# Attention projections as three fp32r products of high and low parts in place of fp32 matmuls

## The chip, the cores and the metric

The kernel runs on one core of a Trainium2 chip. The metric is the device time of one execution in microseconds (us). The profile is of one execution on that core.

## What is computed

The input x has 32 sequences of 256 tokens of width 128. Three layers follow each other, each on the normalised output of the one before and added to it: an expert FFN (weight 0.5), a differential attention, and the same FFN again. The attention, cut to what matters:

```python
q = (x @ Wq.T + bq)   # 256 wide: 16 heads, two streams of 8
k = (x @ Wk.T + bk)   # likewise
v = (x @ Wv.T + bv)   # 128 wide: 16 heads of 8
q1, q2, k1, k2 = rope of the halves of q and k
a1, a2 = softmax(causal(q1 k1^T * scale)), softmax(causal(q2 k2^T * scale))
out = (a1 - lam * a2) @ v
out = out * rsqrt(mean(out^2) + 1e-6) * head_norm_w * (1 - LAMBDA_INIT)
return out @ Wo.T + bo
```

## The kernel before, in words

`build` runs `ffn`, `attention` and `ffn` one after the other. Each is a block of five instruction streams (SyncE's DMA queue, GpSimd, ScalarE, VectorE, TensorE), written out by hand, with semaphores between them. There is no planner: an engine does its work in the order of its code.

The attention goes through the 32 sequences in turns. In a turn, work for several sequences is interleaved: the table `ORDER` lists 33 units of TensorE's work, and `offset(kind, u)` says which sequence a unit is for (+1 is the next one, -3 the third one back). All engines walk `ORDER` in the same way, and `AFTER` says behind which unit an engine does its further pieces of work. Each unit's result goes to one of three PSUM buffers of 1024 columns, `ring[:, pos % 3]`, where `pos` is its place in `ORDER`. `free` makes TensorE wait until the unit three places back has been read; so the pace of one unit is tied to the reader of another.

The units, in the order that matters here, are

```python
ORDER = [("XT", 0), ("T", 6), ("QK", 0), ("NM", 0), ("QK", 1), ("S", 0), ("S", 1), ("T", 7), ("T", 8), ("S", 2),
         ...
         ("S", 6), ("S", 7), ("T", 0), ("V", 0), ("T", 1), ("T", 2), ("NT", 0), ("NT", 1), ("OT", 0), ("S", 8),
         ...
```

- XT turns the normalised input (two 128x128 transposes, L1250). ScalarE copies it to `xt` in SBUF (L996).
- QK 0 and QK 1 are the projections of queries and of keys: four products each, with 128 stationary columns of `wqk` and the 256 columns of `xt` streaming (`mm`, L1223). VectorE reads them in four pieces of 256 columns, adding the bias and multiplying by the rotation (`turned`, L1087). GpSimd and ScalarE split the result in three bf16 parts, and DMAs stack them.
- V is the projection of values: two products, with 128 columns of `xt` stationary and the 128 columns of `wv` streaming. VectorE adds the bias (L1096).
- S is a set of scores whose row maximum VectorE takes (L1108); T is the same scores turned, to which ScalarE applies the exponential (L1002). In the timeline, an S unit is `att_kd,att_qs` with `att_hide`, and a T unit `att_qs,att_kd` with `att_hide_t`.
- "weigh 0" to "weigh 3" are 32 small matmuls each of the probabilities with the values (L1238), and NT turns their result back for VectorE (L1291 and L1116 on). NM turns the maxima (L1304).

An fp32 matmul shows in the trace as two instructions. The FFNs already do their large products with fp32r parts: `PRODUCTS = ((0, 0), (0, 1), (1, 0))` is high times high, high times low and low times high, the high part being a ScalarE copy to fp32r and the low part what VectorE or GpSimd subtracts. In the trace an fp32r operand of a matmul is written f32 as well; the names of the tiles tell them apart.

Before the turns there is a setup: DMAs bring weights and constants, VectorE clears keys and computes `stream_w` (L1184), TensorE waits for masks and weights. The projection of sequence 0 then comes in a turn of its own.

## Time and profile before

| | |
|---|---|
| time, median of 3 runs (lowest to highest) | 1902.27 us (1902.24 to 1903.05) |
| the profiled execution | 1901.86 us, its span 1900.0 us |
| mean granted clock of TensorE | 0.976 |
| TensorE busy | 1700.9 us (90%) |
| VectorE, ScalarE, GpSimd busy | 1368.9, 1275.2, 1048.1 us |

The span is from the first to the last instruction; what the profiled execution's time has beside it lies around it. The attention's first instructions start at about 436 us, and its steady turns run to about 1400 us. Starts are given in us from the span's start. Engines: PE is TensorE's matmuls, PEld its weight loads, DVE VectorE, ACT ScalarE, POOL GpSimd, SP the queue that issues the DMAs. Matmuls overlap, so a record's length is longer than its share of the stream: the distance of two starts tells the pace.

### The profile page before, as it was taken

What the parts mean: (1) busy time and instruction counts of PE and PEld (TensorE: products, weight loads), DVE (VectorE), ACT (ScalarE), POOL (GpSimd) and SP (SyncE); (2) the same over time, 40 slices, a digit from 0 to 9 for tenths busy, and PEclk for the clock granted to TensorE, in tenths of its full rate; (3) what the DMA queues carried; (4) which work ended last, traced back from release to release, by engine and by line L of the source; (5) the groups of instructions that cost most, each with busy time, mean ns of one, the idle gap of its engine ahead of it and who ended that gap; (6) DMA issues with size and microseconds to landing.
All of it is one profiled execution on the core that took longest, in us unless ns stands there. A gap on an engine that the chain in (4) does not pass through costs nothing. (4 is left out here: it accounts for less than half of the span.)

```text
span 1900.0 us, 43151 instructions
## 1 busy us (share of the span) xinstructions
PE 1700.9 (90%) x16448; PEld 1233.5 (65%) x16448; DVE 1368.9 (72%) x3442; ACT 1275.2 (67%) x1613; POOL 1048.1 (55%) x703
## 2 busy tenths in 40 slices
PE   4999999993699999999999999999975599999999
PEld 3778777772456656666666666666643487777787
DVE  5777777765877777777777777777751577777775
ACT  4777777771266676766767666676765577777776
POOL 4888888874333433434334343333411688888885
PEclk9999999996899999999999999999998799999999
DMA  3333333222322323233232322323211223333331
GB/s 111 101 112 112 112 112 101 85 90 80 81 63 78 84 60 92 59 85 82 61 92 58 85 77 68 92 54 89 73 28 51 90 99 111 112 106 107 112 107 62
DMA packets 142434, 163.14 MB, mean 86 GB/s; under 512 B 13218, under 2 KB 124018, under 8 KB 141042
## 3 DMA queue, kind: packets, MB, share of 16 engines
q1 hardware_dynamic: 142228, 160.38, 28.0%
q8 instruction: 131, 2.15, 0.5%
q14 instruction: 75, 0.61, 0.1%
HBM read 91.20 MB, written 14.70 MB: 56 GB/s over the span
## 5 line engine op out<-in xcount | busy, mean ns | idle before, releaser
L1002 ACT ACTIVATE att_prob<-att_ring 128x1024 f32<-128x1024 f32 x384 | 389.1, 1024 | 190.6 <-PE att_ring L1223 185.7
L292 POOL TENSOR_TENSOR ffn_h_low<-ffn_h,ffn_h_high 128x1024 fp32r<-128x1024 f32 x192 | 458.8, 2403 | 95.0 <-ACT ffn_h_high L341 94.8
L1108 DVE TENSOR_REDUCE att_nmax<-att_ring 128x4 f32<-128x1024 f32 (+1 forms) x384 | 454.0, 1218 | 73.0 <-PE att_ring L1223 72.4
L479 DVE TENSOR_TENSOR ffn_h<-ffn_up,ffn_comb_wide 128x1024 f32<-128x1024 f32 x256 | 311.3, 1216 | 125.0 <-ACT ffn_up L334 122.7
L334 ACT ACTIVATE ffn_up<-ffn_up 128x1024 f32<-128x1024 f32 x256 | 258.1, 1008 | 202.8 <-PE ffn_up L567 201.0
L341 ACT ACTIVATE ffn_h_high<-ffn_h 128x1024 fp32r<-128x1024 f32 x256 | 269.3, 1052 | 0.7 <-DVE ffn_h L479 0.7
L918 POOL TENSOR_TENSOR att_qk<-att_turned 128x512 f32<-128x512 f32 x64 | 81.5, 1273 | 321.2 <-DVE att_turned L1087 321.2
L567 PE MATMUL ffn_up<-ffn_xt_high,ffn_w_high 128*128 128x512 f32 x512 | 214.6, 419 | 1.6 <-DVE ffn_h L479 1.5
L580 PE MATMUL ffn_y<-ffn_h_high,ffn_w_high 128*128 128x512 f32 x512 | 205.5, 401 | 7.3 <-POOL ffn_h_low L292 6.0
L284 POOL TENSOR_TENSOR ffn_ez<-ffn_e_const,ffn_nz 128x16 f32<-128x16 f32 x64 | 185.8, 2904 | 38.2 <-DVE ffn_nz L405 38.2
L567 PE MATMUL ffn_up<-ffn_xt_low,ffn_w_high 128*128 128x512 f32 x512 | 203.5, 397 | 0.0
L567 PE MATMUL ffn_up<-ffn_xt_high,ffn_w_low 128*128 128x512 f32 x512 | 203.3, 397 | 0.0
L580 PE MATMUL ffn_y<-ffn_h_low,ffn_w_high 128*128 128x512 f32 x512 | 201.6, 394 | 0.0
L580 PE MATMUL ffn_y<-ffn_h_high,ffn_w_low 128*128 128x512 f32 x512 | 200.0, 391 | 0.0
L1223 PE MATMUL att_ring<-att_qs,att_kd 64*128 64x256 bf16 (+1 forms) x2048 | 150.4, 246 | 52.6 <-DVE att_nmax L1108 29.4
L1238 PE MATMUL att_o_ps<-att_prob,att_v 128*32 128x256 f32 (+1 forms) x4096 | 194.2, 331 | 0.0
L1223 PE MATMUL att_ring<-att_hide,att_eye 64*128 64x256 bf16 (+1 forms) x1536 | 176.2, 308 | 0.0
L1223 PE MATMUL att_ring<-att_hide_t,att_eye 64*128 64x256 bf16 (+1 forms) x1536 | 174.5, 306 | 0.0
L1223 PE MATMUL att_ring<-att_kd,att_qs 64*128 64x256 bf16 (+1 forms) x2048 | 150.7, 246 | 23.3 <-DVE att_nmax L1108 15.6
L1238 PEld LDWEIGHTS att_o_ps<-att_prob,att_v 128*32 128x32 f32 x4096 | 115.3, 110 | 85.9 <-ACT att_prob L1002 26.7
L1087 DVE SCALAR_TENSOR_TENSOR att_turned<-att_ring,att_bqk,att_rope 128x256 f32<-128x256 f32 x256 | 106.2, 477 | 80.4 <-PE att_ring L1223 80.4
L1223 PEld LDWEIGHTS att_ring<-att_qs,att_kd 64*128 64x128 bf16 x2048 | 64.2, 94 | 134.9 <-DVE att_nmax L1108 74.3
(142 smaller groups left out, 2826.8 us busy)
## 6 DMA issues: line engine op xcount, KB each, us to landing
ffn_comb_wide<-ffn_comb_d SPq DMA_DIRECT2D x128, 512.0 KB, 5.6
att_qs<-att_parts SPq DMA_DIRECT2D x192, 128.0 KB, 2.5
att_kd<-att_parts SPq DMA_DIRECT2D x192, 128.0 KB, 2.5
ffn_x<-x SPq DMA_DIRECT2D x32, 256.0 KB, 3.1
ffn_w<-w SPq DMA_DIRECT2D x4, 1024.0 KB, 7.2
x<-ffn_out SPq DMA_DIRECT2D x16, 256.0 KB, 2.4
att_x<-x SPq DMA_DIRECT2D x32, 128.0 KB, 2.3
att_xr<-x SPq DMA_DIRECT2D x32, 128.0 KB, 2.3
```

What stands on the lines that cost most here:

```text
L284: nc.gpsimd.tensor_tensor(ez[:, k].rearrange("p t e -> p (t e)"), e_const[:, 0:n], nz[:, k].rearrange("p t e -> p (t e)"), ALU.pow).then_i ...
L292: nc.gpsimd.tensor_tensor(hts[1][:, e % NH], h[:, e % NH], hts[0][:, e % NH], ALU.subtract).then_inc(low_by_pool, 1)
L334: nc.scalar.activation(up[:, e % NUP], up[:, e % NUP], ACT.Silu).then_inc(silu_ready, 1)
L341: nc.scalar.activation(hts[0][:, e % NH], h[:, e % NH], ACT.Copy).then_inc(high_ready, 1)
L479: nc.vector.tensor_tensor(h[:, e % NH], up[:, e % NUP], comb_wide[:, b.c % NW, e].unsqueeze(1).to_broadcast([P, HE, FT]), ALU.mult).then_i ...
L567: last = nc.tensor.matmul(up[:, e % NUP, k], w1s[a1][:, col:col + P], xts[a2][:, b.slot()], start=(n == 0), stop=(n == 2))
L580: last = nc.tensor.matmul(y[:], w2s[a1][:, col:col + D], hts[a2][:, e % NH, k], start=(e == 0 and k == 0 and n == 0), stop=(e == E - 1 and ...
L1002: nc.scalar.activation(prob[:, u % NP], ring[:, ORDER.index((kind, u)) % 3], ACT.Exp, scale=SCALE).then_inc(prob_ready, 1)
L1087: last = nc.vector.scalar_tensor_tensor(out=turned[:, u, partner, c * S:(c + 1) * S], in0=ring[:, pos % 3, col:col + S], scalar=bqk[:, n:n ...
L1108: nc.vector.tensor_reduce(nmax[:, b, :, h0:h0 + cnt], ring[:, pos % 3] .rearrange("p (s h k) -> p s h k", s=2, k=width), AX.X, ALU.max, ne ...
L1223: return nc.tensor.matmul(out, lhs, rhs, start=start, stop=stop)
L1238: last = nc.tensor.matmul(o_ps[VW * i:VW * (i + 1), g % 2, j, b * P:S], v[:, k, b, h], p, start=(b == 0), stop=(b == 1), tile_position=(0, ...
```

## The change

ScalarE's copy of the turned input goes to an fp32r tile, the high part. VectorE then subtracts it from the PSUM original, giving the low part, and TensorE's QK waits for that (`xt_low`) instead of for the copy. `wqk` and `wv` are split once in the setup, two copies on ScalarE and two subtractions on VectorE, and TensorE waits for these before its first transposes. Each product of QK and of V becomes three fp32r products accumulated in PSUM. The output projection `wo` (OP) stays in fp32.

```diff
--- before.py
+++ after.py
250.31 0.39 PE L567 MATMUL ffn_up<-ffn_xt_high,ffn_w_low 128*128 128x512 f32 x1
...
250.54 0.40 PE L580 MATMUL ffn_y<-ffn_h_high,ffn_w_high 128*128 128x512 f32 x1
...
252.04 0.19 PEld L547 LDWEIGHTS ffn_gate_ps<-ffn_gate_ws,ffn_xt_high 128*128 128x128 f32 x1
...
252.15 -736,7 +736,9 250.31 0.39 PE L567 MATMUL ffn_up<-ffn_xt_high,ffn_w_low 128*128 128x512 f32 x1
...
250.54 0.40 PE L580 MATMUL ffn_y<-ffn_h_high,ffn_w_high 128*128 128x512 f32 x1
...
252.04 0.19 PEld L547 LDWEIGHTS ffn_gate_ps<-ffn_gate_ws,ffn_xt_high 128*128 128x128 f32 x1
...
252.15
         var_eps = sb("var_eps", [P, QB])
         rstd = sb("rstd", [P, QB])
         xn = sb("xn", [P, QB, D])
-        xt = sb("xt", [P, S])
+        wqks = [sb(f"wqk_{n}", [P, 2 * NC4, P], F32R) for n in ("high", "low")]
+        wvs = [sb(f"wv_{n}", [P, D], F32R) for n in ("high", "low")]
+        xts = [sb(f"xt_{n}", [P, S], F32R) for n in ("high", "low")]
         turned = sb("turned", [P, 2, 2, 2 * S])
         qk = sb("qk", [P, 2, 2 * S])
         left = sb("left", [P, 2, 2 * S])
250.31 0.39 PE L567 MATMUL ffn_up<-ffn_xt_high,ffn_w_low 128*128 128x512 f32 x1
...
250.54 0.40 PE L580 MATMUL ffn_y<-ffn_h_high,ffn_w_high 128*128 128x512 f32 x1
...
252.04 0.19 PEld L547 LDWEIGHTS ffn_gate_ps<-ffn_gate_ws,ffn_xt_high 128*128 128x128 f32 x1
...
252.15 -791,6 +793,9 250.31 0.39 PE L567 MATMUL ffn_up<-ffn_xt_high,ffn_w_low 128*128 128x512 f32 x1
...
250.54 0.40 PE L580 MATMUL ffn_y<-ffn_h_high,ffn_w_high 128*128 128x512 f32 x1
...
252.04 0.19 PEld L547 LDWEIGHTS ffn_gate_ps<-ffn_gate_ws,ffn_xt_high 128*128 128x128 f32 x1
...
252.15
         ln_step = sem("ln_step")
         rstd_ready = sem("rstd_ready")
         xn_ready = sem("xn_ready")
+        weight_high = sem("weight_high")
+        weight_low = sem("weight_low")
+        xt_low = sem("xt_low")
         pe = {kind: sem(f"{kind}_computed") for kind in UNITS}
         read = {kind: sem(f"{kind}_read") for kind in UNITS}
         qk_ready = sem("qk_ready")
250.31 0.39 PE L567 MATMUL ffn_up<-ffn_xt_high,ffn_w_low 128*128 128x512 f32 x1
...
250.54 0.40 PE L580 MATMUL ffn_y<-ffn_h_high,ffn_w_high 128*128 128x512 f32 x1
...
252.04 0.19 PEld L547 LDWEIGHTS ffn_gate_ps<-ffn_gate_ws,ffn_xt_high 128*128 128x128 f32 x1
...
252.15 -982,6 +987,9 250.31 0.39 PE L567 MATMUL ffn_up<-ffn_xt_high,ffn_w_low 128*128 128x512 f32 x1
...
250.54 0.40 PE L580 MATMUL ffn_y<-ffn_h_high,ffn_w_high 128*128 128x512 f32 x1
...
252.04 0.19 PEld L547 LDWEIGHTS ffn_gate_ps<-ffn_gate_ws,ffn_xt_high 128*128 128x128 f32 x1
...
252.15
             @block.scalar
             def _(act):
 
+                act.wait_ge(weights_in, 16 * 12)
+                nc.scalar.activation(wqks[0][:], wqk[:], ACT.Copy).then_inc(weight_high, 1)
+                nc.scalar.activation(wvs[0][:], wv[:], ACT.Copy).then_inc(weight_high, 1)
                 act.wait_ge(dve_setup, 2)
                 nc.scalar.activation(ln_ms[:], y0[:], ACT.Ln).then_inc(lam_ready, 1)
                 act.wait_ge(lam_sums, 1)
250.31 0.39 PE L567 MATMUL ffn_up<-ffn_xt_high,ffn_w_low 128*128 128x512 f32 x1
...
250.54 0.40 PE L580 MATMUL ffn_y<-ffn_h_high,ffn_w_high 128*128 128x512 f32 x1
...
252.04 0.19 PEld L547 LDWEIGHTS ffn_gate_ps<-ffn_gate_ws,ffn_xt_high 128*128 128x128 f32 x1
...
252.15 -993,7 +1001,7 250.31 0.39 PE L567 MATMUL ffn_up<-ffn_xt_high,ffn_w_low 128*128 128x512 f32 x1
...
250.54 0.40 PE L580 MATMUL ffn_y<-ffn_h_high,ffn_w_high 128*128 128x512 f32 x1
...
252.04 0.19 PEld L547 LDWEIGHTS ffn_gate_ps<-ffn_gate_ws,ffn_xt_high 128*128 128x128 f32 x1
...
252.15
                             wait_unit(act, turn, kind, u)
 
                             wait(act, pe["V"], turn.at(0, 1, 1))
-                            nc.scalar.activation(xt[:], ring[:, ORDER.index((kind, u)) % 3, 0:S],
+                            nc.scalar.activation(xts[0][:], ring[:, ORDER.index((kind, u)) % 3, 0:S],
                                                  ACT.Copy).then_inc(read["XT"], 1)
                         if kind == "T" and turn.runs(offset(kind, u)):
                             wait_unit(act, turn, kind, u)
250.31 0.39 PE L567 MATMUL ffn_up<-ffn_xt_high,ffn_w_low 128*128 128x512 f32 x1
...
250.54 0.40 PE L580 MATMUL ffn_y<-ffn_h_high,ffn_w_high 128*128 128x512 f32 x1
...
252.04 0.19 PEld L547 LDWEIGHTS ffn_gate_ps<-ffn_gate_ws,ffn_xt_high 128*128 128x128 f32 x1
...
252.15 -1133,6 +1141,11 250.31 0.39 PE L567 MATMUL ffn_up<-ffn_xt_high,ffn_w_low 128*128 128x512 f32 x1
...
250.54 0.40 PE L580 MATMUL ffn_y<-ffn_h_high,ffn_w_high 128*128 128x512 f32 x1
...
252.04 0.19 PEld L547 LDWEIGHTS ffn_gate_ps<-ffn_gate_ws,ffn_xt_high 128*128 128x128 f32 x1
...
252.15
                             wait(dve, ms_ready, turn.at(-3, 1, 1))
                             nc.vector.tensor_scalar(ms_eps[:], ms[:], 1.0 / HD, RMS_EPS, ALU.mult,
                                                     ALU.add).then_inc(norm_step, 1)
+                        if kind == "XT" and turn.runs(1):
+
+                            wait(dve, read["XT"], turn.at(1, 1, 1))
+                            nc.vector.tensor_tensor(xts[1][:], ring[:, pos % 3, 0:S], xts[0][:],
+                                                    ALU.subtract).then_inc(xt_low, 1)
                         if (kind, u) == AFTER["newton"] and turn.runs(-3):
 
                             wait(dve, rms_step, turn.at(-3, 2, 2))
250.31 0.39 PE L567 MATMUL ffn_up<-ffn_xt_high,ffn_w_low 128*128 128x512 f32 x1
...
250.54 0.40 PE L580 MATMUL ffn_y<-ffn_h_high,ffn_w_high 128*128 128x512 f32 x1
...
252.04 0.19 PEld L547 LDWEIGHTS ffn_gate_ps<-ffn_gate_ws,ffn_xt_high 128*128 128x128 f32 x1
...
252.15 -1184,6 +1197,9 250.31 0.39 PE L567 MATMUL ffn_up<-ffn_xt_high,ffn_w_low 128*128 128x512 f32 x1
...
250.54 0.40 PE L580 MATMUL ffn_y<-ffn_h_high,ffn_w_high 128*128 128x512 f32 x1
...
252.04 0.19 PEld L547 LDWEIGHTS ffn_gate_ps<-ffn_gate_ws,ffn_xt_high 128*128 128x128 f32 x1
...
252.15
                 nc.vector.scalar_tensor_tensor(out=stream_w[:, :, 1], in0=by_head(1), scalar=-LAMBDA_INIT,
                                                in1=by_head(0), op0=ALU.add, op1=ALU.subtract).then_inc(lam_step, 1)
                 dve.wait_ge(lam_step, 3)
+                dve.wait_ge(weight_high, 2)
+                nc.vector.tensor_tensor(wqks[1][:], wqk[:], wqks[0][:], ALU.subtract).then_inc(weight_low, 1)
+                nc.vector.tensor_tensor(wvs[1][:], wv[:], wvs[0][:], ALU.subtract).then_inc(weight_low, 1)
                 dve.wait_ge(v_set, 1)
                 body(first.after())
                 clear_keys(1)
250.31 0.39 PE L567 MATMUL ffn_up<-ffn_xt_high,ffn_w_low 128*128 128x512 f32 x1
...
250.54 0.40 PE L580 MATMUL ffn_y<-ffn_h_high,ffn_w_high 128*128 128x512 f32 x1
...
252.04 0.19 PEld L547 LDWEIGHTS ffn_gate_ps<-ffn_gate_ws,ffn_xt_high 128*128 128x128 f32 x1
...
252.15 -1197,6 +1213,7 250.31 0.39 PE L567 MATMUL ffn_up<-ffn_xt_high,ffn_w_low 128*128 128x512 f32 x1
...
250.54 0.40 PE L580 MATMUL ffn_y<-ffn_h_high,ffn_w_high 128*128 128x512 f32 x1
...
252.04 0.19 PEld L547 LDWEIGHTS ffn_gate_ps<-ffn_gate_ws,ffn_xt_high 128*128 128x128 f32 x1
...
252.15
                 te.wait_ge(masks_in, 16 * 3)
                 tile = [slice(TILE * s, TILE * (s + 1)) for s in range(2)]
                 te.wait_ge(weights_in, 16 * 12)
+                te.wait_ge(weight_low, 2)
 
                 def free(turn, pos):
 
250.31 0.39 PE L567 MATMUL ffn_up<-ffn_xt_high,ffn_w_low 128*128 128x512 f32 x1
...
250.54 0.40 PE L580 MATMUL ffn_y<-ffn_h_high,ffn_w_high 128*128 128x512 f32 x1
...
252.04 0.19 PEld L547 LDWEIGHTS ffn_gate_ps<-ffn_gate_ws,ffn_xt_high 128*128 128x128 f32 x1
...
252.15 -1212,7 +1229,9 250.31 0.39 PE L567 MATMUL ffn_up<-ffn_xt_high,ffn_w_low 128*128 128x512 f32 x1
...
250.54 0.40 PE L580 MATMUL ffn_y<-ffn_h_high,ffn_w_high 128*128 128x512 f32 x1
...
252.04 0.19 PEld L547 LDWEIGHTS ffn_gate_ps<-ffn_gate_ws,ffn_xt_high 128*128 128x128 f32 x1
...
252.15
                         if before.runs(offset(kind, u)):
                             break
                         back -= 3
-                    if kind == "T":
+                    if kind == "XT":
+                        wait(te, xt_low, before.at(1, 1, 1))
+                    elif kind == "T":
                         wait(te, prob_ready, before.at(offset(kind, u), 12, u + 1))
                     elif kind == "NT":
                         wait(te, norm_step, before.at(offset(kind, u), NORM, 3 * u + 3))
250.31 0.39 PE L567 MATMUL ffn_up<-ffn_xt_high,ffn_w_low 128*128 128x512 f32 x1
...
250.54 0.40 PE L580 MATMUL ffn_y<-ffn_h_high,ffn_w_high 128*128 128x512 f32 x1
...
252.04 0.19 PEld L547 LDWEIGHTS ffn_gate_ps<-ffn_gate_ws,ffn_xt_high 128*128 128x128 f32 x1
...
252.15 -1249,12 +1268,16 250.31 0.39 PE L567 MATMUL ffn_up<-ffn_xt_high,ffn_w_low 128*128 128x512 f32 x1
...
250.54 0.40 PE L580 MATMUL ffn_y<-ffn_h_high,ffn_w_high 128*128 128x512 f32 x1
...
252.04 0.19 PEld L547 LDWEIGHTS ffn_gate_ps<-ffn_gate_ws,ffn_xt_high 128*128 128x128 f32 x1
...
252.15
                                 for t in range(QB):
                                     last = nc.tensor.transpose(buf[:, t * P:(t + 1) * P], xn[:, t], ident[:])
                             elif kind == "QK":
-                                wait(te, read["XT"], turn.at(1, 1, 1))
+                                wait(te, xt_low, turn.at(1, 1, 1))
                                 for n in range(4):
-                                    last = mm(buf[:, n * S:(n + 1) * S], wqk[:, 4 * u + n], xt[:])
+                                    for i, (a1, a2) in enumerate(PRODUCTS):
+                                        last = mm(buf[:, n * S:(n + 1) * S], wqks[a1][:, 4 * u + n], xts[a2][:],
+                                                  start=(i == 0), stop=(i == 2))
                             elif kind == "V":
                                 for t in range(QB):
-                                    last = mm(buf[:, t * D:(t + 1) * D], xt[:, t * P:(t + 1) * P], wv[:])
+                                    for i, (a1, a2) in enumerate(PRODUCTS):
+                                        last = mm(buf[:, t * D:(t + 1) * D], xts[a2][:, t * P:(t + 1) * P], wvs[a1][:],
+                                                  start=(i == 0), stop=(i == 2))
                             elif kind == "S":
                                 k = turn.slot(0)
                                 if u == 0:
```

## Rows read from the trace of the kernel before

**Rows 1.** The page: busy time, share of the span and instructions of each engine.
```profile
PE 1700.9 (90%) x16448; PEld 1233.5 (65%) x16448; DVE 1368.9 (72%) x3442; ACT 1275.2 (67%) x1613; POOL 1048.1 (55%) x703
```

**Rows 2.** Windows of the attention: busy PE, PEld, DVE, ACT, POOL; granted clock; DMA.
```profile
1200.00:1300.00 100.00, 92.44 (x1309) 61.47 (x1310) 77.96 (x156) 69.13 (x90) 34.98 (x38) 1.00 0.28 74
```

**Rows 3.** Timeline of TensorE: the XT transposes of two turns, fifteen turns apart.
```profile
908.05 0.44 PE L1250 MATMUL att_ring<-att_ident,att_xn 128*128 128x128 f32 x2
...
1355.17 0.44 PE L1250 MATMUL att_ring<-att_ident,att_xn 128*128 128x128 f32 x2
```

**Rows 4.** Timeline of all engines, from the XT copy on: start, us, engine, line, [idle before <-releaser].
```profile
908.68 0.38 ACT L996 ACTIVATE att_xt<-att_ring 128x256 f32<-128x256 f32 x1
...
909.20 1.97 PE L1223 MATMUL att_ring<-att_xt,att_wqk 128*128 128x256 f32 x8 [0.17 <-ACT att_xt L996]
...
911.00 0.27 PE L1304 MATMUL att_ring<-att_ident,att_nmax_parts 128*96 128x128 bf16 x2
...
911.11 1.95 PE L1223 MATMUL att_ring<-att_xt,att_wqk 128*128 128x256 f32 x8
911.20 1.66 DVE L1087 SCALAR_TENSOR_TENSOR att_turned<-att_ring,att_bqk,att_rope 128x256 f32<-128x256 f32 x4 [2.24 <-PE att_ring L1223]
...
913.10 1.66 DVE L1087 SCALAR_TENSOR_TENSOR att_turned<-att_ring,att_bqk,att_rope 128x256 f32<-128x256 f32 x4 [0.24 <-PE att_ring L1223]
...
914.67 2.35 DVE L1108 TENSOR_REDUCE att_nmax<-att_ring 128x8 f32<-128x1024 f32 x2
...
914.81 0.39 PE L1223 MATMUL att_ring<-att_qs,att_kd 64*128 64x256 bf16 x4 [0.34 <-DVE att_turned L1087]
...
918.32 4.73 DVE L1108 TENSOR_REDUCE att_nmax<-att_ring 128x8 f32<-128x1024 f32 x4 [0.37 <-PE att_ring L1223]
```

**Rows 5.** The same timeline, from V to the reads of NT.
```profile
926.91 0.71 PE L1223 MATMUL att_ring<-att_wv,att_xt 128*128 128x128 f32 x4
...
927.93 0.49 DVE L1096 TENSOR_TENSOR att_v<-att_ring,att_bv 128x128 f32<-128x128 f32 x2
...
928.23 0.59 PE L1223 MATMUL att_ring<-att_hide_t,att_eye 64*128 64x512 bf16 x4
...
928.75 1.97 PE L1291 MATMUL att_ring<-att_ident,att_o_t 128*128 128x128 f32 x16
929.88 0.36 DVE L1116 RECIPROCAL att_rsum<-att_ring 128x32 f32<-128x32 f32 x1 [1.46 <-PE att_ring L1291]
```

**Rows 6.** Timeline of TensorE and its weight loads in the first FFN: fp32r products.
```profile
250.31 0.39 PE L567 MATMUL ffn_up<-ffn_xt_high,ffn_w_low 128*128 128x512 f32 x1
...
250.54 0.40 PE L580 MATMUL ffn_y<-ffn_h_high,ffn_w_high 128*128 128x512 f32 x1
...
252.04 0.19 PEld L547 LDWEIGHTS ffn_gate_ps<-ffn_gate_ws,ffn_xt_high 128*128 128x128 f32 x1
...
252.15 0.19 PEld L547 LDWEIGHTS ffn_gate_ps<-ffn_gate_ws,ffn_xt_low 128*128 128x128 f32 x1
```

**Rows 7.** VectorE's groups by line and shape: count, busy us, mean ns of one.
```profile
L487 DVE TENSOR_TENSOR ffn_h_low<-ffn_h,ffn_h_high 128x1024 fp32r<-128x1024 f32 x24 | 29.9, 1244 | 0.0
...
L395 DVE TENSOR_TENSOR ffn_xt_low<-ffn_turn_ps,ffn_xt_high 128x512 fp32r<-128x512 f32 x12 | 8.3, 692 | 17.2 <-ACT ffn_xt_high L322 17.2
...
L1127 DVE TENSOR_TENSOR att_xo<-att_ring,att_xrb 128x256 f32<-128x256 f32 x28 | 11.6, 415 | 0.0
```

**Rows 8.** Timeline of the attention's setup.
```profile
441.97 0.43 SPq L828 DMA_DIRECT2D att_lam_in<-lk  x1
...
454.19 0.18 DVE L1184 SCALAR_TENSOR_TENSOR att_stream_w<-att_lam_exp 128x16 f32<-128x16 f32 x1
...
454.48 5.26 PE L1223 MATMUL att_ring<-att_xt,att_wqk 128*128 128x256 f32 x16 [2.72 <-ACT att_xt L996]
458.17 3.27 DVE L1087 SCALAR_TENSOR_TENSOR att_turned<-att_ring,att_bqk,att_rope 128x256 f32<-128x256 f32 x8 [3.80 <-PE att_ring L1223]
```

**Rows 9.** Busy time by window, first QK projection: columns as in rows 2.
```profile
455.00:459.00 4.00, 4.00 (x14) 3.24 (x13) 0.83 (x3) 0.00 (x0) 0.00 (x0) 0.67 0.03 6
```

## Prediction

> **What bounds the kernel now.** I read first the page's busy shares [rows 1], then the busy time of each engine and the granted clock in the attention stage alone [rows 2]. The reader should see there that TensorE is the busiest engine (92 of 100 us), but that VectorE has 78 of 100 too, so neither can be taken as the bound over a whole turn. The granted clock is 1.00, the 2.4 GHz level, in the steady part. The stage is strictly periodic: the transposes of the turned input (XT) start at 908.05 in one turn and at 1355.17 fifteen turns later, 447.12 / 15 = 29.81 us a turn [rows 3]. Only what makes this period longer or shorter counts, some 28 times; the first three turns and the setup are to be costed apart.
>
> So I read the timeline of one turn around the edited lines [rows 4, 5] and asked in each place who waits last. From the XT copy on, TensorE computes QK 0 (909.20 to 911.17), VectorE starts to read it at once (911.20, after 2.24 us idle), TensorE computes QK 1 (ready 913.06), VectorE has read QK 0 at 912.86, waits 0.24 us and reads QK 1 until 914.76, and only then can TensorE start T 7 (914.81), whose PSUM buffer that was. From T 7 on TensorE runs through weigh 1, T 8 and S 2 with no gap to speak of, until VectorE, idle again, gets S 2 at 918.32 [rows 4]. Whatever moves T 7 moves the turn. The second place is V: it streams at 926.91, T 1 and T 2 follow, then the NT transposes at 928.75, and VectorE has been idle for 1.46 us when it starts on them at 929.88 [rows 5]. There TensorE is the path, so whatever V takes longer is lost. The V result itself has slack: it is ready at 927.62, and VectorE takes it at 927.93, being occupied until then with the statistics. Between these places the path lies on VectorE's maxima and on TensorE's weighing, which the change does not touch.
>
> **The change, part by part.** Times are those of the turn shown.
>
> *Queries and keys, duration.* Before, one fp32 product is recorded as two instructions, and 8 take 1.80 us from first start (909.20) to the start of what follows (911.00): 0.216 each, and 0.07 once, at the beginning. The result is there 0.17 us after the stream's end (911.17) [rows 4]. After, a unit has 12 fp32r instructions of 256 columns. No row has that shape. Lower bound: the loads of fp32r weights follow each other every 0.11 us in the gate's products, where only 16 columns stream (252.04, 252.15) [rows 6], so 0.111. Upper bound: fp32r with 512 columns follows every 0.23 us (250.31, 250.54) [rows 6], where 512 columns at 2.4 GHz are 0.213; if those 17 ns are a fixed cost, 256 columns take 0.107 + 0.017 = 0.124; if they are in proportion, 0.115. I take 0.117. The stream is 0.07 + 12 x 0.117 = 1.47 us instead of 1.80: -0.33 (bounds -0.40 and -0.25) for each unit.
>
> *Queries and keys, a later start.* The low part is a VectorE subtraction that stands between ACT's copy and the first product. The copy ends at 909.06 [rows 4]. VectorE has nothing to do then: its last piece before is the mean square, and what is queued behind the new wait is the read of QK 0 itself, so nothing else is held up. Its price: the same operation on 512 columns of PSUM takes 0.692 us, and an add of 256 columns from PSUM (L1127) 0.415; I take 0.42 [rows 7]. It starts 0.03 after the copy (as 911.20 stands to 911.17), ends at 909.51, and TensorE starts 0.07 to 0.14 later (0.05 at T 7, 0.14 at the present first product): first product 909.58 to 909.65, or +0.41 (0.38 to 0.45).
>
> *What comes out at T 7.* QK 0 is ready 0.41 - 0.33 = 0.08 later, so VectorE starts on it at 911.28. Its four reads take 1.57 when another operation follows without a wait (from 913.10 to the reduction that comes next, 914.67), so it can begin QK 1 at 912.85. TensorE has QK 1 at 911.08 (stream end) + 0.11 (NM) + 1.95 - 0.32 = 912.82. Both agree: the read begins at 912.86 instead of 913.10, **-0.24 us**. With the lower bounds of both terms -0.35; with the upper ones QK 1 is ready at 913.03 and the gain is -0.03. Of 0.65 us of stream saved in two units, then, 0.41 goes to the subtraction, and the rest is the 0.24 that VectorE now waits. S 0 is no limit: it needs QK 0's buffer, now free 0.08 later, and its reduction stands behind QK 1's in any case.
>
> *V.* 4 instructions become 6. With 128 columns the stationary loads set the pace: 4 of them and their set-in fill 926.91 to 927.56 [rows 5], and both kinds of load come every 0.11 us [rows 6]. So 2 x 0.111 = **+0.22 us**, with nothing to hide it, as said above; the result is then ready at 927.84, still ahead of VectorE's 927.93.
>
> *Sum of a turn:* -0.24 + 0.22 = -0.02, times 28 = -0.6 us. Bounds: -0.35 + 0.21 = -0.14 (-3.9 us), and -0.03 + 0.23 = +0.20 (+5.6 us).
>
> *Setup and cold turns.* ACT's two weight copies wait for the weights alone, whose last DMA is issued at 441.97 [rows 8]; ACT has nothing else that is needed before 453.9, so I cost them at nothing (if the weights were late, up to 1.3 us). VectorE's two subtractions come behind its last setup step, which ends at 454.37 [rows 8]: 1.24 for 1024 columns [rows 7] and about 0.2 for 128, until 455.85. TensorE now waits for them ahead of the first XT, which was hidden before. Transposes 0.66, copy 0.37, subtraction 0.42 and the gaps bring the first product to about 457.5 instead of 454.48: +3.0. The clock there is 0.67 and below [rows 9], so the 8 instructions took 458.17 - 454.48 = 3.69 us; 12 at half clock, 0.222 each, take about 3.1: -0.6. QK 1 hides behind VectorE. That leaves +2.4, and -0.2 for each of two more cold turns (+0.42 - 0.6): **+2.0 us**, between +1 (the POOL and DMA chain of the first turns takes up some) and +3.5.
>
> *Sum:* -0.6 + 2.0 = +1.4 on the profiled execution's 1901.86 (span 1900.0 and 1.9 around it) gives 1903.3; the median of the runs shown is 0.4 higher, so **1903.7**. By the bounds: -2.9 and +9.1, or 1899.4 to 1911.4.
>
> **The rivals.** A difference under 0.2% (3.8 us) is about what a measurement of this kernel can't tell from none.
>
> *V's narrow fp32r products are slow.* Nothing shows how fast fp32r streams with 128 columns; gate rows with 16 and FFN rows with 512 leave it open. If an instruction takes as long as a 256-column fp32 one, 0.216, V takes 6 x 0.216 + 0.2 instead of 0.65: +0.85, a net +0.61 us a turn, 28 x 0.61 + 2 = +19: 1921. It decides from 0.125 us an instruction on, where V's extra passes 0.30 and the turn's net (3.8 - 2) / 28 = 0.064. For it: only that the width is untried. Against: two widths ran without such a penalty. Chance 0.08.
>
> *The upper bounds hold (fixed cost, late wake-up).* QK gains 0.03 to 0.1, V costs 0.22: 28 x 0.15 + 2.5 = +6.7: 1909. Chance 0.2.
>
> *V's extra 0.22 us is absorbed (the other side).* If NT is in truth held by something other than the stream before it (the label on its idle load is VectorE's V read, 928.42, which is 0.33 ahead of 928.75), only the QK gain is left: 28 x -0.24 + 2.0 = -4.7: 1897.5. It needs 0.21 us a turn net to count as faster. Against: T 2's last four matmuls start at 928.23; of 512 columns each, two at a time, they stream 0.43 us at 2.4 GHz, so until 928.66, and NT follows 0.09 later [rows 5]. Chance 0.09.
>
> *TensorE's saving counts in full.* The Trainium skill, "FP8 and Floating Point Precision", section "TensorE Precision Notes", has true FP32 as four passes, so that three products would cost three quarters of it; the 256-column rows agree (two times 0.216 are four times 0.107). As a mechanism of this kernel: if all three projections fell to three quarters, 3.46 + 0.43 us a turn would fall by 0.97, less the subtraction 0.41: -0.56, times 28, +2 = -14: 1888.5. Against: V is bound by loads, and VectorE's back-to-back reads cap QK. Chance 0.02.
>
> *fp32r weights load faster in the attention.* If a load took half of 0.111, V's six instructions would take 0.33 us instead of 0.44, so -0.11 in place of +0.22, and the turn -0.35: 28 x -0.35 + 2 = -7.8: 1894.5. It decides from 0.079 an instruction down, where the turn's net passes -0.21. Against: the gate loads the same type and shape at 0.11 [rows 6]. Chance 0.01. The Trainium skill, "TensorE: Matmul & The Clock Gate", section "Weight-path perf modes", speaks for it: it has the fast weight load on for 128 weights of any type that is not FP32. By this rule, the trace does not agree for fp32r.
>
> *The forecast*, no measurable change, by the sum above: chance 0.60.
>
> **How the numbers follow.** The forecast is the likeliest case, 1903.7. Slower by over 0.2% (above 1906.1): the first two rivals, 0.28, and 0.02 for a dearer setup: 0.30. Faster (below 1898.5): 0.12 together, of which 0.02 may stay within: 0.10. Same: 0.60. The range 1899 to 1911, the bounds of the unknown costs, leaves out the slow V (0.08) and most of the three faster cases (0.10); the case of the upper bounds is inside.
>
> **What would show it.** Right: QK 0's twelve matmuls span about 1.6 us; first product some 0.4 us later after the XT copy; VectorE's wait between the QK reads gone; QK matmul starts 0.115 to 0.124 apart; V's group about 0.9 us long; the period 29.7 to 30.0; the first QK product near 457.5. Wrong: matmul starts in V over 0.13 apart, NT's distance to the S units before it unchanged, a period under 29.65, or a subtraction much longer than 0.42 because ACT's exponential reads PSUM beside it.

## The result, and the profile after

The change costs 7.8 us: a median of 1910.09 us (1909.79 to 1910.46, 6 runs) against 1902.26 us (6 runs), a ratio of 1.0038 with a 95% interval of 1.0025 to 1.0051. That is above the forecast of 1903.7 and inside its range of 1899 to 1911; the outcome is "slower by over 0.2%", to which 0.30 was given. The profiled execution has a span of 1908.7 us, 8.7 above the one before. (In the diff above, rows of the first FFN's timeline, those of [rows 6], stand where the line numbers of each piece belong; they are no part of the kernel.)

The page's busy shares answer to [rows 1]:

```profile
PE 1693.1 (89%) x16768; PEld 1245.2 (65%) x16768; DVE 1381.3 (72%) x3476; ACT 1276.0 (67%) x1615; POOL 1047.1 (55%) x703
```

The window of the steady turns, with the columns of [rows 2]:

```profile
1200.00:1300.00 100.00, 91.34 (x1362) 62.46 (x1360) 79.40 (x160) 66.83 (x88) 37.13 (x42) 1.00 0.32 85
```

TensorE's busy time falls by 7.8 us, and the program is longer by as much. The timeline of TensorE has the XT transposes of two turns, fifteen apart, to be laid beside [rows 3]:

```profile
914.94 0.44 PE L1269 MATMUL att_ring<-att_ident,att_xn 128*128 128x128 f32 x2
...
1362.55 0.44 PE L1269 MATMUL att_ring<-att_ident,att_xn 128*128 128x128 f32 x2
```

447.61 / 15 = 29.84 us a turn, +0.03. Over the steady turns that is under 1 us of the 8.7. So where are the others? The starts of XT, read from the same view of both executions, tell it:

| us from the span's start | before | after | difference |
|---|---|---|---|
| first XT | 451.11 | 455.88 | +4.77 |
| second XT | 468.69 | 471.38 | +2.69 |
| third XT | 494.35 | 500.25 | +5.90 |
| fifth XT | 550.35 | 556.84 | +6.49 |
| last XT | 1355.17 | 1362.55 | +7.38 |
| first instruction of the second FFN | 1464.69 | 1473.74 | +9.05 |
| end of the span | 1900.0 | 1908.7 | +8.7 |

Three quarters come ahead of the fifth XT: 2.7 us in the first projection and its chain, 3.2 us more from the second XT to the third, and 0.6 from there to the fifth. The steady turns add 0.9. After the last XT, where one QK and one V are all that is left of the changed code, 1.7 us are added.

The QK stretch of the turn at 914.94, all engines, answers to [rows 4]:

```profile
915.57 0.38 ACT L1004 ACTIVATE att_xt_high<-att_ring 128x256 fp32r<-128x256 f32 x1
...
915.98 0.43 DVE L1147 TENSOR_TENSOR att_xt_low<-att_ring,att_xt_high 128x256 fp32r<-128x256 f32 x1
...
916.55 0.36 PE L1242 MATMUL att_ring<-att_xt_high,att_wqk_high 128*128 128x256 f32 x1 [0.63 <-DVE att_xt_low L1147]
...
916.75 0.28 PE L1242 MATMUL att_ring<-att_xt_low,att_wqk_high 128*128 128x256 f32 x1
...
916.86 0.28 PE L1242 MATMUL att_ring<-att_xt_high,att_wqk_low 128*128 128x256 f32 x1
...
918.06 0.27 PE L1327 MATMUL att_ring<-att_ident,att_nmax_parts 128*96 128x128 bf16 x2
...
918.26 3.25 DVE L1095 SCALAR_TENSOR_TENSOR att_turned<-att_ring,att_bqk,att_rope 128x256 f32<-128x256 f32 x8 [1.86 <-PE att_ring L1242]
...
921.57 0.39 PE L1242 MATMUL att_ring<-att_qs,att_kd 64*128 64x256 bf16 x4
```

The reader should see three things. TensorE starts QK 0 at 1.61 us after XT (916.55 - 914.94) instead of 1.15, having waited for the subtraction. The whole unit streams until NM at 918.06, 1.51 us instead of 1.80, so QK 0 is with VectorE 0.17 us later after XT than before (3.32 against 3.15). And VectorE's eight reads are now one unbroken piece of 3.25 us, the 0.24 us of waiting between them gone. T 7 starts 6.63 after XT, before 6.76: 0.13 us are won.

V and the first NT transposes, which answer to [rows 5]:

```profile
933.67 0.33 PE L1242 MATMUL att_ring<-att_wv_high,att_xt_high 128*128 128x128 f32 x1
...
934.28 0.27 PE L1242 MATMUL att_ring<-att_wv_low,att_xt_high 128*128 128x128 f32 x1
...
934.68 0.49 DVE L1104 TENSOR_TENSOR att_v<-att_ring,att_bv 128x128 f32<-128x128 f32 x2
...
935.16 0.59 PE L1242 MATMUL att_ring<-att_hide_t,att_eye 64*128 64x512 bf16 x4
...
935.68 1.53 PE L1314 MATMUL att_ring<-att_ident,att_o_t 128*128 128x128 f32 x12
```

From V's start to NT's it is 2.01 us, before 1.84: the 0.17 us by which V is longer arrive in full at NT. -0.13 + 0.17 is the +0.03 of the period, but for the rounding of the starts.

The large new piece is in the second projection, at the start of the turns. VectorE and ScalarE there, and TensorE's first product:

```profile
471.61 1.76 DVE L1177 MEMSET att_kd<- 128x2048 uint32 x1 [0.38 <-issue]
472.08 0.38 ACT L1004 ACTIVATE att_xt_high<-att_ring 128x256 fp32r<-128x256 f32 x1 [3.71 <-PE att_ring L1269]
...
473.75 1.76 DVE L1177 MEMSET att_kd<- 128x2048 uint32 x1 [0.37 <-issue]
475.43 0.36 DVE L1147 TENSOR_TENSOR att_xt_low<-att_ring,att_xt_high 128x256 fp32r<-128x256 f32 x1
...
475.94 0.55 PE L1242 MATMUL att_ring<-att_xt_high,att_wqk_high 128*128 128x256 f32 x1 [3.90 <-DVE att_xt_low L1147]
```

The copy is ready at 472.46, but the subtraction stands in VectorE's queue behind two clears of key slots, and TensorE waits for it, 3.90 us in all; the first product is 4.56 us after XT (471.38). Before, the same clears ran beside the products, and the first product was 1.22 us after XT:

```profile
468.69 0.66 PE L1250 MATMUL att_ring<-att_ident,att_xn 128*128 128x128 f32 x2 [6.48 <-DVE att_xn L1067]
468.92 1.76 DVE L1164 MEMSET att_kd<- 128x2048 uint32 x1 [0.37 <-issue]
...
469.91 4.60 PE L1223 MATMUL att_ring<-att_xt,att_wqk 128*128 128x256 f32 x10 [0.56 <-ACT att_xt L996]
...
471.06 1.76 DVE L1164 MEMSET att_kd<- 128x2048 uint32 x1 [0.38 <-issue]
```

### The profile page after: what moved, and what is told of

It is laid out like the page before. It is cut to its first block and busy times, and to the rows that moved or that the text cites. A ratio compares the mean times of both kernels' runs of the same rounds, so it can differ in the third digit from the quotient of the medians.

```text
span 1908.7 us, 43829 instructions
## 1 busy us (share of the span) xinstructions
PE 1693.1 (89%) x16768; PEld 1245.2 (65%) x16768; DVE 1381.3 (72%) x3476; ACT 1276.0 (67%) x1615; POOL 1047.1 (55%) x703
```

## The experiments

All kernels below start from the changed kernel, except e5, which starts from the one before. Ratios are to the kernel before. "..." marks what is left out of an edit.

**e1: the key clears behind the subtraction**

```diff
                 body(first.after())
-                clear_keys(1)
-                clear_keys(2)
                 turns(body, 0)
...
                             nc.vector.tensor_tensor(xts[1][:], ring[:, pos % 3, 0:S], xts[0][:],
                                                     ALU.subtract).then_inc(xt_low, 1)
+                            if turn.c <= 0:
+                                clear_keys(turn.c + 2)
```

> The changed kernel, with VectorE's two clears of key slots 1 and 2 (1.76 us each) issued behind the low-part subtraction of the first two projections instead of ahead of the turns. Theory: most of the loss is there, because in the second projection the subtraction (475.43) stood in VectorE's queue behind both clears (471.61 to 475.5) while the copy was ready at 472.46. Then the second projection's first product comes some 3 us sooner relative to its XT (1.6 us after it instead of 4.56), and the time falls by about 3 us, from 1910.1 to 1907. Rival: the first turns are longer because the clock is at 1.2 GHz there and 24 loads cost as much as 16 long streams; then moving the clears gives under 0.5 us.

1906.74 us, ratio 1.0024 (1.0013 to 1.0034), 3.35 us less than the changed kernel. The theory's number. But the profiled execution was the longest of the eight (1912.06 us), and its fourth XT came 30.92 us after the third, where the changed kernel needs 26.98. So the same kernel was run once more.

**e9: the same kernel once more**

> The kernel with the key clears behind the subtraction once more, for another look at its first turns: in the profile already taken the distance from the third to the fourth XT was 30.92 us against 26.98 without the edit, while most of its timed runs were short. Theory: that is the clock's phase, and another execution has the third distance near 27 and the time near 1906.5. Rival: it is a wait that the edit brings, and both profiles have it.

1905.37 us, ratio 1.0017 (1.0007 to 1.0028), 4.7 us less than the changed kernel; the two medians of this one kernel differ by 1.4 us, so the 3.35 is not exact. Its second projection, TensorE, ScalarE and VectorE:

```profile
471.98 0.38 ACT L1004 ACTIVATE att_xt_high<-att_ring 128x256 fp32r<-128x256 f32 x1 [3.71 <-PE att_ring L1269]
472.40 0.42 DVE L1150 TENSOR_TENSOR att_xt_low<-att_ring,att_xt_high 128x256 fp32r<-128x256 f32 x1 [1.26 <-ACT att_xt_high L1004]
472.97 0.55 PE L1242 MATMUL att_ring<-att_xt_high,att_wqk_high 128*128 128x256 f32 x1 [1.02 <-DVE att_xt_low L1150]
```

The first product is 1.69 us after XT (471.28), as the theory said, and the third XT comes 25.52 after the second, where the changed kernel needs 28.87: 3.35 us less. In the execution of e1 it was 26.34, or 2.5 us less. From the third to the fourth it is 26.99 here (496.80 to 523.79). The same stretch in windows, for this execution (the last three columns are granted clock, DMA share and GB/s):

```profile
497.00:524.00 27.00, 19.49 (x236) 13.20 (x234) 21.62 (x39) 9.39 (x13) 7.68 (x7) 0.87 0.26 71
```

And for the execution of e1:

```profile
498.00:529.00 31.00, 23.75 (x236) 15.89 (x234) 21.89 (x39) 9.54 (x13) 7.68 (x7) 0.72 0.23 62
```

Equal work (236 matmuls, 39 VectorE instructions in both), a granted clock of 0.87 against 0.72, and 4.3 us more of TensorE's busy time for it (19.49 and 23.75). So the odd 30.92 goes with that execution's clock and not with the edit.

**e4: TensorE waits for the split weights at the first QK**

```diff
-                te.wait_ge(weight_low, 2)
...
                             elif kind == "QK":
+                                if turn.c == -1 and u == 0:
+                                    te.wait_ge(weight_low, 2)
                                 wait(te, xt_low, turn.at(1, 1, 1))
```

> The changed kernel with TensorE's wait for the split weights at the first QK instead of ahead of the first XT. Theory: the first XT is hidden again, VectorE goes from the weights' subtraction straight to the input's, and the first product comes at about 456.1 instead of 457.5: -1.4 us, 1908.7. Rival: the chain of GpSimd and DMAs behind the first projection takes it up, and the time stays at 1910.

1908.39 us, ratio 1.0028 (1.0017 to 1.0038), 1.7 less than the changed kernel. XT is hidden again, VectorE goes straight from the weights to the input, and the first product is at 456.04:

```profile
454.13 1.22 DVE L1201 TENSOR_TENSOR att_wqk_low<-att_wqk,att_wqk_high 128x1024 fp32r<-128x1024 f32 x1
455.28 0.28 DVE L1202 TENSOR_TENSOR att_wv_low<-att_wv,att_wv_high 128x128 fp32r<-128x128 f32 x1
455.48 0.42 DVE L1147 TENSOR_TENSOR att_xt_low<-att_ring,att_xt_high 128x256 fp32r<-128x256 f32 x1
456.04 0.55 PE L1241 MATMUL att_ring<-att_xt_high,att_wqk_high 128*128 128x256 f32 x1 [4.54 <-DVE att_xt_low L1147]
```

**e8: both edits of the start (e1 and e4)**

> The changed kernel with the two edits of its start alone: key clears behind the subtraction and the late wait for the split weights; the steady turns are untouched (29.84). Theory: they add, 3.35 + 1.7 measured one by one, so 1905.0; what then stands above the kernel before, about 2.5 us, is 28 times 0.03 and the lower clock of the first turns and the drain. Rival: both remove the same wait, and the time stays at 1906.5 or above.

1904.65 us, ratio 1.0017 (1.0007 to 1.0027), 5.4 less than the changed kernel and 3.7 less than e4: they add, as nearly as these medians can tell. What remains above the kernel before is 2.4 us.

**e2: V with two products**

This leaves out the product with the low part of V's weights.

```diff
                                 for t in range(QB):
-                                    for i, (a1, a2) in enumerate(PRODUCTS):
+                                    for i, (a1, a2) in enumerate(PRODUCTS[:2]):
...
-                                                  start=(i == 0), stop=(i == 2))
+                                                  start=(i == 0), stop=(i == 1))
```

> The changed kernel with two products for V instead of three (the low part of its weights is left out): 4 instructions as in the kernel before. Theory: V is on TensorE's path, and loads set its pace, so each turn loses 0.22 us: the period falls from 29.84 to 29.62 and the time by 28 x 0.22 = 6 us to 1904. Rival: V's extra time is absorbed ahead of NT, and the period stays within 0.05 of 29.84.

The period, from TensorE's timeline, is (1356.77 - 912.52) / 15 = 29.62:

```profile
912.52 0.44 PE L1269 MATMUL att_ring<-att_ident,att_xn 128*128 128x128 f32 x2
...
1356.77 0.44 PE L1269 MATMUL att_ring<-att_ident,att_xn 128*128 128x128 f32 x2
```

1902.32 us, ratio 1.0003 (0.9993 to 1.0012). Two instructions fewer of 0.11 us each take exactly 0.22 us off every turn. V's time is on the path. The time fell by 7.8 us, 1.6 more than 28 x 0.22; from the last XT to the second FFN this execution took 108.65 us, the one of the changed kernel 111.19, and of these 2.5 us the edit explains 0.22.

**e3: the low input's products last**

```diff
-                                wait(te, xt_low, turn.at(1, 1, 1))
-                                for n in range(4):
-                                    for i, (a1, a2) in enumerate(PRODUCTS):
-                                        last = mm(..., wqks[a1][:, 4 * u + n], xts[a2][:],
-                                                  start=(i == 0), stop=(i == 2))
+                                wait(te, read["XT"], turn.at(1, 1, 1))
+                                for i, (a1, a2) in enumerate(((0, 0), (1, 0), (0, 1))):
+                                    if i == 2:
+                                        wait(te, xt_low, turn.at(1, 1, 1))
+                                    for n in range(4):
+                                        last = mm(..., wqks[a1][:, 4 * u + n], xts[a2][:],
+                                                  start=(i == 0 and n % 2 == 0), stop=(i == 2 and n % 2 == 1))
```

(The four pieces are taken in pairs: an accumulation group is opened with the first piece of a pair and closed with the second, since their products now alternate.)

> The changed kernel with QK's products in another order: high times high and low weights times high input for all four pieces first, waiting only for ScalarE's copy, and only then the low input's products, behind the wait for the subtraction. Theory: the subtraction costs the path 0.46 us a turn (first product 1.61 after XT against 1.15 before the change), and 8 products of 0.12 cover it; the period falls by 0.46 to 29.38, the time by 28 x 0.46 = 13 us and a bit in the first turns, to 1896: faster than both kernels. Rival: VectorE's reads of QK and not the start of QK 0 set T 7; then the period moves by under 0.1.

1892.81 us, ratio 0.9948 (0.9931 to 0.9964): 9.7 us faster than the kernel before and 17.3 faster than the changed one. A turn of it, all engines:

```profile
904.80 0.44 PE L1269 MATMUL att_ring<-att_ident,att_xn 128*128 128x128 f32 x2
...
905.84 0.42 DVE L1147 TENSOR_TENSOR att_xt_low<-att_ring,att_xt_high 128x256 fp32r<-128x256 f32 x1
...
905.96 0.71 PE L1242 MATMUL att_ring<-att_xt_high,att_wqk_high 128*128 128x256 f32 x4 [0.17 <-ACT att_xt_high L1004]
906.51 0.64 PE L1242 MATMUL att_ring<-att_xt_high,att_wqk_low 128*128 128x256 f32 x4
906.98 0.64 PE L1242 MATMUL att_ring<-att_xt_low,att_wqk_high 128*128 128x256 f32 x4
...
907.66 3.25 DVE L1095 SCALAR_TENSOR_TENSOR att_turned<-att_ring,att_bqk,att_rope 128x256 f32<-128x256 f32 x8 [1.40 <-PE att_ring L1242]
...
910.97 0.39 PE L1242 MATMUL att_ring<-att_qs,att_kd 64*128 64x256 bf16 x4
```

The subtraction (905.84 to 906.26) lies beneath the first eight products, which run until 906.98. T 7 starts 6.17 after XT, not 6.63, and the period is (1345.51 - 904.80) / 15 = 29.38. All 0.46 us arrive.

That is 28 x 0.46 = 12.9 of the 17.3 us. Most of the others are won ahead of the fourth XT, which comes at 523.10 and not at 527.23. In the second projection the subtraction still stands behind the two clears, but eight products go ahead of it, and TensorE waits for it for 1.20 us instead of 3.90:

```profile
475.47 1.22 PE L1242 MATMUL att_ring<-att_xt_low,att_wqk_high 128*128 128x256 f32 x4 [1.20 <-DVE att_xt_low L1147]
```

From the third XT to the fourth 1.5 us are won as well; the granted clock was 0.94 there (497 to 524), and 0.87 in the changed kernel (500 to 527), so not all of that need be the edit's.

**e5: fp32 products and the subtraction alone**

The kernel before with one more VectorE operation, whose result nothing reads:

```diff
+                        if kind == "XT" and turn.runs(1):
+                            wait(dve, read["XT"], turn.at(1, 1, 1))
+                            nc.vector.tensor_tensor(xt_low_sb[:], ring[:, pos % 3, 0:S], xt[:],
+                                                    ALU.subtract).then_inc(xt_low, 1)
...
-                                wait(te, read["XT"], turn.at(1, 1, 1))
+                                wait(te, xt_low, turn.at(1, 1, 1))
```

> The kernel before, with fp32 projections, and beside them the new subtraction alone: VectorE writes the difference of the PSUM original and the copy to a tile that nothing reads, and QK waits for it as in the changed kernel. Theory: the subtraction is 0.46 us on the path of every turn, so the period rises from 29.81 to 30.27; in the second projection it stands behind the two key clears and costs 3.3 us more; 28 x 0.46 + 3.3 = +16 us, 1918. Rival for the first turns (the fp32r work at the low clock is what costs): the second projection's first product stays within 2 us of its XT. Rival for the steady turns (VectorE's time, not the wait, counts): the period stays under 29.9.

1922.3 us, ratio 1.0103 (1.0086 to 1.012): 19.6 us for one operation of 0.43 us a turn and its wait, 3.6 more than expected. The period is (1374.23 - 920.23) / 15 = 30.27 as expected. The excess is in the first turns, and goes with a lower granted clock there: the second XT comes 1.8 us later than before (470.52), with 0.50 and 0.67 granted in 455 to 459 and 459 to 462 (before: 0.67 and 1.00); from the third to the fourth XT it is 28.13 us instead of 26.41, at 0.80 (498 to 525) instead of 0.87 (494 to 521). The second projection, with no fp32r in it, shows the same wait behind the clears:

```profile
472.89 1.76 DVE L1171 MEMSET att_kd<- 128x2048 uint32 x1 [0.38 <-issue]
474.57 0.36 DVE L1141 TENSOR_TENSOR att_xt_low<-att_ring,att_xt 128x256 fp32r<-128x256 f32 x1
475.08 2.47 PE L1232 MATMUL att_ring<-att_xt,att_wqk 128*128 128x256 f32 x5 [3.90 <-DVE att_xt_low L1141]
```

So both prices, in the steady turn and in the second projection, belong to the subtraction and not to the fp32r products.

**e6: V in fp32 again**

```diff
+                            nc.vector.tensor_copy(xt[:], ring[:, pos % 3, 0:S]).then_inc(xt_low, 1)
...
                                 for t in range(QB):
-                                    for i, (a1, a2) in enumerate(PRODUCTS):
-                                        last = mm(..., xts[a2][:, t * P:(t + 1) * P], wvs[a1][:],
-                                                  start=(i == 0), stop=(i == 2))
+                                    last = mm(buf[:, t * D:(t + 1) * D], xt[:, t * P:(t + 1) * P], wv[:])
```

> The changed kernel with V in fp32 again: VectorE copies the turned input to an fp32 tile behind the subtraction, while it waits for QK 0. Theory: V is back at 4 instructions and costs 0.22 us less, the copy of about 0.4 us is hidden in VectorE's idle 1.8 us; period 29.62, time 1904. Rival: the copy delays VectorE's reads of QK; period 29.84 or more.

(The split of `wv` in the setup is gone too.) 1904.63 us, ratio 1.0011 (1.0002 to 1.0021). The period is 29.67, not 29.62: from V's first start to what follows, the four fp32 instructions take 0.65 us (931.08 to 931.73), the four fp32r ones of e2 0.60 (931.24 to 931.84). The difference is at the beginning, where the first two starts are 0.21 us apart in fp32 and 0.17 in fp32r. The fp32r V costs 0.17 us a turn against fp32, and the copy is hidden.

**e7: all four edits together**

> The changed kernel with all four edits: the low input's products last, V in fp32 with VectorE's copy, the key clears behind the subtraction, the late wait for the split weights. Theory: the parts add, since each lies at another place of the path: period 29.38 - 0.22 = 29.16; time 1892.8 - 6.2 - 3.3 - 1.4 = 1882. Rival: with T 7 earlier another wait takes over (S 1 behind the read of NM, T 9 behind ScalarE's exponential), the period stays at 29.3 or above, and the time at 1886 or above.

1884.72 us, ratio 0.9898 (0.9881 to 0.9914): the fastest, 17.9 us ahead of the kernel before. The period is (1336.84 - 898.84) / 15 = 29.20, within 0.01 of 29.38 less the 0.17 of e6: the parts add in the steady turns, and no other wait took over. Of the 2.7 us above what this run was expected to take, 28 x 0.04 = 1.1 are V's. The rest may be the stretch behind the last XT, which took 111.4 us in the profiled execution and 109.5 in that of e8. One thing differs from the edits taken one by one: the wait for the split weights stands behind the first four products, not ahead of them. The first product of all comes at 454.13 us, and the second XT at 468.90, 0.2 later than before.

## Why the prediction was right or wrong

**The places.** Right: T 7 sets the turn by way of VectorE's reads of QK, and V sets it by way of NT. e3 and e5 moved the first by 0.46 us and the period followed to 0.01; e2 moved the second by 0.22 and the period followed in full, so the rival by which V's time is absorbed falls. The forecast of the period, -0.02 us a turn, stands against +0.03.

**QK's duration.** The second and the twelfth start of a unit (916.75 and 917.94) are ten steps of 0.119 us apart, between the bounds of 0.111 and 0.124 and next to the 0.117 that was taken; the first step is 0.20. The unit is 1.51 us long and not 1.47. (The upper bound's -0.25 should read -0.24.)

**The subtraction.** 0.43 us by itself (0.42 forecast), and the first product 0.46 later (0.41, upper bound 0.45): right in kind, a little small. With both misses QK 0 is ready 0.17 us later and not 0.08, and the gain at T 7 is 0.13 instead of 0.24. VectorE's wait between its reads is gone, as forecast; they follow each other with no gap, and QK 0's end alone sets T 7.

**V.** The loads do set the pace, 0.11 us apart (933.83, 933.94, 934.05 in TensorE's timeline). Two more cost 0.22 (e2), but V's four fp32 instructions took 0.05 us more than four of fp32r (e6), so 0.17 was the difference. The rival of slow narrow fp32r products did not come: 128 columns go at the loads' pace. Nor did faster loads: these fp32r loads, too, come every 0.11 us, and so do the fp32 loads of V before, so the rule of the Trainium skill on the fast weight load ("TensorE: Matmul & The Clock Gate", "Weight-path perf modes") is not borne out for fp32r here.

**Three passes against four.** QK's stream is 12 x 0.119 = 1.43 us where it was 8 x 0.216 = 1.73, that is 0.83 and not 0.75. The count of passes by the Trainium skill ("FP8 and Floating Point Precision", "TensorE Precision Notes") holds for the columns, 256 at 2.4 GHz being 0.107, but each fp32r instruction takes some 12 ns more than that. As a mechanism for the time it was rightly given little: of 0.58 us saved in two units, 0.13 reached T 7.

**Setup, first projection.** Right: first product at 457.54 (457.5 forecast), VectorE begins to read at 460.51 instead of 458.17, +2.3 (+2.4), and the second XT is 2.7 late. That "QK 1 hides behind VectorE" was not quite so; VectorE waits 0.30 us for it, where its eight reads were one piece before [rows 8], and that is the difference of 2.7 and 2.4:

```profile
460.51 1.66 DVE L1095 SCALAR_TENSOR_TENSOR att_turned<-att_ring,att_bqk,att_rope 128x256 f32<-128x256 f32 x4 [3.02 <-PE att_ring L1242]
462.47 1.66 DVE L1095 SCALAR_TENSOR_TENSOR att_turned<-att_ring,att_bqk,att_rope 128x256 f32<-128x256 f32 x4 [0.30 <-PE att_ring L1242]
```

e4 gave 1.7 us of it back.

**The step that failed** is the cold turns, costed at "-0.2 for each of two more cold turns". The second projection costs +3.2 and the next stretch +0.6. For the steady turn the prediction had asked what is queued behind the new wait and found nothing; it did not ask what stands ahead of the subtraction in VectorE's queue in the turn where that is not the steady work. The two key clears were 3.5 us that used to run beside the products. Moving them took 3.35 us off in e1, 4.7 in e9 and 3.7 in e8 against e4, TensorE's wait fell from 3.90 to 1.02 us, and e5 shows the same 3.90 in fp32. The stretch behind the last XT was given no term at all; it was 1.7 longer.

**What was luck.** 1910.1 lies inside the range, but not for the range's reasons. Its upper end was made of 5.6 us from the steady turns and 3.5 from the setup and the cold turns; measured are 0.9 in the steady turns, 6.5 in the setup and the cold turns, and 1.7 behind the last XT. Nor was the rival "the upper bounds hold", which gives 1909, what happened: it asks for 0.15 us a turn, and 0.03 came. The likeliest case, a difference under 0.2%, did not come, and most of the 0.30 for "slower" rested on that rival.

**The rest.** With both edits of the start undone (e8), 2.4 us remain. In its profiled execution the second XT is still 1.7 us later than before (470.37 against 468.69), the fourth 2.6 and the last 3.3. So the larger part is the first projection: the subtractions on VectorE hold the first product until 456.24 (454.48 before), and then VectorE waits for QK 1:

```profile
456.24 0.55 PE L1241 MATMUL att_ring<-att_xt_high,att_wqk_high 128*128 128x256 f32 x1 [4.54 <-DVE att_xt_low L1150]
...
459.18 1.66 DVE L1098 SCALAR_TENSOR_TENSOR att_turned<-att_ring,att_bqk,att_rope 128x256 f32<-128x256 f32 x4 [0.95 <-PE att_ring L1241]
461.45 1.66 DVE L1098 SCALAR_TENSOR_TENSOR att_turned<-att_ring,att_bqk,att_rope 128x256 f32<-128x256 f32 x4 [0.61 <-PE att_ring L1241]
```

In e7, where the first four products wait for neither subtraction, this loss is down to 0.2 us. The steady turns give 27 x 0.03 = 0.8, and 0.9 lie between the second XT and the fourth.

There the granted clock changes between its two levels, 1.2 and 2.4 GHz. In a window of 51 us around the second and third XT it was 0.80 in the kernel before (465 to 516):

```profile
465.00:516.00 51.00, 31.82 (x282) 20.74 (x282) 38.68 (x61) 9.78 (x15) 18.27 (x18) 0.80 0.37 97
```

and 0.76 in the changed kernel, whose third XT is 5.9 us later (471 to 522):

```profile
471.00:522.00 51.00, 31.91 (x296) 22.47 (x298) 38.55 (x62) 9.15 (x14) 15.36 (x14) 0.76 0.36 96
```

TensorE had been idle for 3.90 us ahead of the second projection in the changed kernel, and 0.56 before; that the lower clock comes from there is not shown. From the second XT to the third it cost nothing that shows: e9 needed 25.52 us with 0.72 granted (471 to 497), the kernel before 25.66 with 0.81 (468 to 494). From the third to the fourth the changed kernel and e9 need 0.6 us more than before, at 0.87 in all three; what these are is left open.

Behind the last XT the time goes with the execution's clock. The stretch up to the second FFN took 108.65 us in e2 and 108.85 in e4, with a granted clock of 0.98 over its first 100 us; 109.5 in the kernel before and in e8 (0.97); 110.65 in e3 and 111.2 in the changed kernel (0.95); 111.4 in e7 (0.93). e1, e4, e8 and e9 have the changed kernel's code there and took 108.85 to 109.9. So the 1.7 us are not the work of that code; but the changed kernel's six times agree within 0.7 us, and why it should get the lower clock there is left open.

## What to carry to other kernels

A hand-over from ScalarE to TensorE that becomes one through a second engine puts that engine's whole queue into the path: look at what stands ahead of the new operation in every turn, the first ones too, and not only at what waits behind it. When a product is split in parts, issue first the parts whose operands are there first: here 8 of 12 instructions needed nothing of the new operation, and that order alone turned a loss of 7.8 us into a gain of 9.7. Where the moving side has only 128 columns, three fp32r products cost more than one fp32 product (here 0.17 us for two of each): they bring three weight loads of 0.11 us where the fp32 product brings two.

## What the runs showed of the hardware that was not expected

fp32r instructions with 256 columns follow each other every 0.119 us while their weight loads run beneath them, and with 128 columns every 0.11, as with 16 columns in the gate's products [rows 6]. That the load is what limits the two narrow cases is read from this: an eighth of the columns saves nothing. In the first turns, the same 236 matmuls took 27 us at a mean granted clock of 0.87 in one execution and 31 us at 0.72 in another of the same kernel, so a single profile can show 4 us there that the timed runs mostly do not have.
